# Residual stream kept transposed, with the FFN result added to the output rows by accumulating scatters

## What is computed

```
# conditioning: each sequence b has its own 32x32 matrix, picked by index
c = einsum('bct,bcd->bdt', x, weights[subjects])
# attention on c: 32 heads of 16, rope on q and k, causal softmax over 32 positions
q, k, v = c @ wq.T, c @ wk.T, c @ wv.T
x1 = x + attention(rope(q), rope(k), v) @ wo.T
# a linear layer with 8 low-rank experts of rank 16, two of them picked per token
logits = x1 @ Wr.T + 5 * onehot(language)
gates = softmax over the top 2 of logits
x2 = x1 @ W.T + 2 * einsum('bter,bte,eor->bto', x1 @ A, gates, B)
# block FFN: 16 blocks of 32 features, of permuted features; the result goes back
t = x2[:, perm];  t = gelu(t by blocks @ up);  t = t @ down by blocks
out = x1 + t[:, argsort(perm)]
```

## Time and profile before

| | |
|---|---|
| median of 3 runs | 265.93 us (265.58 to 266.53) |
| profiled execution: its own time | 266.65 us |
| its span in the profile | 264.8 us |
| PE busy | 233.0 us, 88% |
| DVE, ACT, POOL busy | 163.5, 118.4, 91.9 us |
| DMA | 11.66 MB |

### The profile page before, as it was taken

One profiled execution on the slowest core, in us unless ns is written; L12 is line 12 of the kernel. 1 busy time (PEld: TensorE's weight loads), 2 busy tenths in 40 slices (PEclk: granted clock), 3 DMA queues, 4 the chain that ended last, 5 costly groups with the idle time before them and its releaser, 6 DMA issues.

```text
span 264.8 us, 5842 instructions
## 1 busy us (share of the span) xinstructions
PE 233.0 (88%) x2472; PEld 194.6 (73%) x2472; DVE 163.5 (62%) x328; ACT 118.4 (45%) x199; POOL 91.9 (35%) x76
## 2 busy tenths in 40 slices
PE   5999498997779999998989999989996888969775
PEld 5999376985558899876867999757685666739543
DVE  2651999999835778848437977484479704424313
ACT  3332456640603234868024248681324599203470
POOL 8259763384920016768000058590001400000000
PEclk9999899997979999999999999999999579979999
DMA  7698421000000000000220000000100000020002
GB/s 229 215 339 280 149 50 57 2 0 0 4 0 0 2 2 1 4 2 0 82 79 2 2 0 2 0 2 26 57 2 0 0 4 0 2 79 2 0 0 79
DMA packets 7529, 11.66 MB, mean 44 GB/s; under 512 B 2032, under 2 KB 2704, under 8 KB 7504
## 3 DMA queue, kind: packets, MB, share of 16 engines
q1 hardware_dynamic: 6784, 9.81, 10.8%
q0 software_dynamic: 432, 1.48, 1.7%
q10 hardware_dynamic: 288, 0.01, 0.1%
HBM read 9.07 MB, written 2.23 MB: 43 GB/s over the span
## 4 chain that ended last, share of the span: by engine, by line
PE 50%; DVE 19%; ACT 11%; DMA 10%; issue 7%; POOL 2%; DVEq 0%; ACTq 0%; SPq 0%; POOLq 0%
PE ps_F L474 7%; PE ps_F L476 7%; PE ps_F L475 6%; PE ps_F L680 6%; ACT pbd L818 5%; PE ps_A L474 5%; PE ps_A L476 4%; PE ps_A L475 4%; DMA rows<-kr 3%; PE ps_F L653 3%; ACT act L900 2%; DMA wg<-rows 2%; PE ps_S L548 2%; PE ps_F L566 2%; PE ps_A L501 1%
## 5 line engine op out<-in xcount | busy, mean ns | idle before, releaser
L436 POOL TENSOR_TENSOR pr<-pr,small 128x512 f32<-128x512 f32 x16 | 16.6, 1048 | 86.7 <-DVE small L1103 86.7
L818 ACT ACTIVATE pbd<-pr 32x512 f32<-32x512 f32 x64 | 40.2, 628 | 9.8 <-DVE pr L1109 5.0
L818 ACT ACTIVATE x<-ps_F 128x512 fp32r<-128x512 f32 (+1 forms) x22 | 13.1, 597 | 49.1 <-PE ps_F L587 35.5
L412 POOL TENSOR_TENSOR rot<-rot,cst 128x512 f32<-128x512 f32 x14 | 18.0, 1288 | 20.2 <-DVE rot L1059 20.2
L1081 DVE TENSOR_TENSOR kbd<-kr,cst 128x512 f32<-128x512 f32 x16 | 20.8, 1342 | 3.6 <-POOL kr L416 3.5
L427 POOL TENSOR_TENSOR kbd<-kr,cst 128x512 f32<-128x512 f32 x16 | 21.1, 1346 | 2.7 <-PE ps_F L483 2.6
L474 PE MATMUL ps_A<-wvT,xc 128*128 128x512 f32 x32 | 14.8, 464 | 5.8 <-DVE wvT L1018 3.5
L1011 DVE TENSOR_TENSOR y<-ps_S,y 128x512 fp32r<-128x512 f32 x8 | 5.5, 688 | 22.8 <-ACT y L818 22.7
L474 PE MATMUL ps_A<-xc,wqT 128*128 128x256 f32 x64 | 18.2, 284 | 1.3 <-DVE xc L1011 1.3
L474 PE MATMUL ps_A<-xc,wkT 128*128 128x256 f32 x64 | 18.3, 286 | 0.0
L474 PE MATMUL ps_F<-x,w2T 128*128 128x256 f32 x64 | 18.3, 286 | 0.0
(11 more groups left out here) (156 smaller groups left out, 643.8 us busy)
## 6 DMA issues: line engine op xcount, KB each, us to landing
xs<-in_x SPq DMA_DIRECT2D x4, 512.0 KB, 4.5
out<-xs SPq DMA_DIRECT2D x3, 512.0 KB, 2.8
pbd<-in_L_attn_wq SPq DMA_DIRECT2D x2, 512.0 KB, 5.2
act<-in_L_attn_wk SPq DMA_DIRECT2D x1, 1024.0 KB, 5.6
act<-in_L_attn_wv SPq DMA_DIRECT2D x1, 1024.0 KB, 8.6
act<-in_L_attn_wo SPq DMA_DIRECT2D x1, 1024.0 KB, 8.0
out<-xs SPq DMA_DIRECT2D x2, 256.0 KB, 2.0
x<-in_L_cond_A SPq DMA_DIRECT2D x1, 256.0 KB, 8.2
```

The source lines that it names most:

```text
L412: pool.tensor_tensor(rv, rv, con("sin").unsqueeze(1).to_broadcast([P, 2 * N // T, T]), ALU.mult).then_inc(rot_sin, 1)
L436: pool.tensor_tensor(pr[:, i, :, :], pr[:, i, :, :], mx[:, i, :].unsqueeze(2).to_broadcast([P, NH // 2, T]), ALU.mult).then_inc(normed, 1)
L818: return sc.activation(dst, src, ACT.Copy)
```

## The change

The host gives x a second time, transposed (`xT`), and turns the output back. The output tensor in memory has one row for each feature of a group: 4 x 512 rows of 256 tokens.

1. `wo_proj(g, i)` makes features 256 i to 256 i + 255 for all 256 tokens of the group: 24 products of 256 columns in place of 12 of 512. It needs the split attention output of both tiles. `add_x` adds into `xt` (two buffers, loaded by SP); `x1_out` and `x1_lo` split `xt` directly. `turn_x1` goes.
2. SP writes `xt` (x1) to the output. The FFN result `y` is copied from PSUM by ACT alone, and POOL adds it to the output rows in memory with four indirect DMAs a group (`add_rows`), by `row_at`, the permuted row numbers. `unpermute`, `unperm`, `y_lo` and `add_ffn` go.
3. x of groups 2 and 3 is loaded without waiting for output. `attn` now lies in the buffer `xc`.
4. In the setup: ACT splits wv ahead of its part of `blocks(1)`; ACT's copies of wo move ahead of `v_out(0, 0)`; the lo part of wo moves from DVE to POOL, behind the first two `norm`; POOL clears `pbd` behind its first `k_blocks`; DVE's order in pass 0 is another, with the splits of the two small weights at its end.
5. In pass 3 PE runs all of pv before the second half of `ffn_down`, and then both halves of `wo_proj`.
6. `lora_down` takes the first two chunks of x1 for both of its products, then the other two.

```diff
+            def load_xt(g):
+                sp.dma_start(xt[:, g % 2, :, :], xT[g]).then_inc(d_xt[g], 16)
...
             for g in range(G):
-                for t in range(GT):
-                    wait_read(sp, Fi(g, "UN", t))
...
+                for i in range(2):
+                    wait_read(sp, Fi(g, "WO", i))
+                sp.dma_start(out_d[g], xt[:, g % 2, :, :]).then_inc(d_x1[g], 16)
...
+            def wo_los():
+
+                for h in range(2):
+                    rows = slice(2 * h, 2 * h + 2)
+                    pool.wait_ge(w_hi, W_AT["wo"] + h + 1)
+                    pool.tensor_tensor(WT["wo"][:, 1, rows, :], raw["wo"][:, rows, :],
+                                       WT["wo"][:, 0, rows, :].bitcast(F32), ALU.subtract).then_inc(wo_lo, 1)
+
+            def add_rows(g):
+
+                pool.wait_ge(rows_ready, G)
+                pool.wait_ge(d_x1[g], 16)
+                for c in range(KC):
+                    wait_read(pool, S_down(g, c // 2))
+                    pool.indirect_dma_start(out=out, out_offset=bass.IndirectOffsetOnAxis(
+                                                ap=row_at[:, g, c:c + 1], axis=0),
+                                            in_=y[:, c, :], in_offset=None, compute_op=ALU.add
+                                            ).then_inc(d_out[g], 16)
...
-            def wo_proj(g, t):
-                it = Fi(g, "WO", t)
-                wait_free(pe, it)
-                wait_read(pe, PVi(g, t))
...
+            def wo_proj(g, i):
+                it = Fi(g, "WO", i)
                 wait_free(pe, it)
                 for t in range(GT):
+                    wait_read(pe, PVi(g, t))
+                W, o = WT["wo"], attn
+                for h in range(2):
+                    c = 2 * i + h
+                    for k in range(KC):
+                        last = mm3(bank(it)[:, N * h:N * h + N],
+                                   W[:, 0, k, P * c:P * c + P], W[:, 1, k, P * c:P * c + P],
+                                   o[:, 0, k, :], o[:, 1, k, :], k == 0, k == KC - 1)
...
             w_his("wk", raw["wk"], WT["wk"], (d_w["wk"], None))
+            w_his("wv", raw["wv"], WT["wv"], (d_w["wv"], None))
             blocks(1)
-            w_his("wv", raw["wv"], WT["wv"], (d_w["wv"], None))
...
-            def x1_out(g, t):
-                split_hi(Fi(g, "XT", t), x1[:, 0, :, P * t:P * t + P], x1_hi)
+            def x1_out(g, i):
+
+                wait_read(sc, Fi(g, "WO", i))
+                copy(x1[:, 0, 2 * i:2 * i + 2, :], xt[:, g % 2, 2 * i:2 * i + 2, :]).then_inc(x1_hi, 1)
```

More of the change, by code:

```diff
@@ L41 @@
 HG = HC // 2
-XS = 3
+XS = 2
 MASKED = -1.0e30
@@ L77, in constants, with build @@
     return c
-def build(nc, x, who, wcond, wq, wk, wv, wo, w2b, wr, wa, up, down, perm, consts, cols, rows, out):
+def build(nc, x, xT, who, wcond, wq, wk, wv, wo, w2b, wr, wa, up, down, perm, consts, rows, out):
     ctx = ExitStack()
@@ L669, in ffn_down @@
                     last.then_inc(s_full(it), 1)
-            def unpermute(g, t, halves=(0, 1)):
-                it = Fi(g, "UN", t)
-                for i in halves:
-                    if i == 0:
-                        wait_free(pe, it)
-                    wait_read(pe, S_down(g, i))
-                    for c in (2 * i, 2 * i + 1):
-                        for part in range(2):
-                            last = pe.matmul(bank(it)[:, :], y2[:, part, c, P * t:P * t + P], unperm[:, c, :],
-                                             start=(c == 0 and part == 0), stop=(c == KC - 1 and part == 1),
-                                             skip_group_check=True)
-                    if i == 1:
-                        last.then_inc(s_full(it), 1)
             def keep_busy(n):
@@ L774, in _ @@
                     pv(g, 0, 3)
+                    for c in range(KC):
+                        pv(g, 1, c)
                     ffn_down(g - 1, 2)
@@ L777, in _ @@
                 wo_proj(g, 0)
-                if not more:
-                    pv(g, 1, 0)
-                    pv(g, 1, 1)
-                    unpermute(g - 1, 0)
-                    turn_x1(g, 0)
-                    pv(g, 1, 2)
-                    pv(g, 1, 3)
-                    unpermute(g - 1, 1)
                 wo_proj(g, 1)
-                if more:
-                    turn_x1(g, 0)
                 if g == 0:
@@ L808, in _ @@
                 ffn_down(G - 1, c)
-            for half in range(2):
-                for t in range(GT):
-                    unpermute(G - 1, t, (half,))
         @block.scalar
@@ L965, in _ @@
                     y_out(g - 1, 0)
-                if more:
-                    probs_block(g, 1, 0)
-                o_out(g, 0)
-                if more:
+                probs_block(g, 1, 0)
+                if more and g:
+                    o_out(g, 0)
                     v_out(g + 1, 0)
-                if g:
                     y_out(g - 1, 1)
-                if not more:
-                    probs_block(g, 1, 0)
+                elif more:
+                    v_out(g + 1, 0)
+                    o_out(g, 0)
+                else:
+                    o_out(g, 0)
                 probs_block(g, 1, 1)
@@ L977, in _ @@
                     v_out(g + 1, 1)
-                else:
-                    x1_out(g, 0)
                 o_out(g, 1)
-                if more:
-                    x1_out(g, 0)
-            x1_out(G - 1, 1)
+                if not more:
+                    y_out(g - 1, 1)
+                x1_out(g, 0)
+                x1_out(g, 1)
             h_out(G - 1)
```

226 lines of the change are left out of this document (101 added, 125 removed).

## The result

The changed kernel took **253.69 us** (median of 4 runs, 253.23 to 254.5) against 265.75 (264.51 to 266.53) for the kernel before on the same chip: ratio 0.9553, 95% interval 0.9508 to 0.9598. The profiled execution took 253.85 with a span of 252.1 us; before, 266.65 with 264.8. 12.1 us went. The forecast was 16.9, and the missing part is what the experiments are about.

What follows compares the result with a forecast made beforehand. PE, busy 88% of the span, was taken as the bound, with DVE and POOL deciding up to 86 us. Terms -12.2 - 4.1 - 3.3 - 0.5 + 1.5 + 1.7 = -16.9 gave 249.7 profiled, 249.0 median; range 244 to 257.

Steps and rivals of the forecast that it cites:

- The clock: PE at three ends of passes: new idle time lowers the clock at one of the three, +1.7 us.
- clock falls at every end: Rival: clock falls at every pass end and stays low in the last group, two more times 1.7, 252.5 us; chance 0.14.
- Group 0: Setup and group 0: reordered setup and earlier splits start `lora_down` at 74.0 instead of 86.25, -12.2 us.
- the first scores come about 5.0 us earlier: Setup: with wv first, DVE's subtractions fill idle times and PE's k, ended by 26.1, bounds group 0's last rope.
- wo on POOL at nothing: Setup: wo's two operations, 5.2 us together, hide in POOL's wait of 6.22 us, costing 0.
- The POOL rival: Group 0: POOL's wo operations and DVE's block each other, the ropes start late, +7, 256 us; chance 0.12.
- Pass 1: End of pass 1: `unpermute` traded for a wait -1.9, transposes -0.9, x's wait -1.27; together -4.1 us.
- Pass 2: End of pass 2: -1.9 and -0.9 as in pass 1, and -0.5 of waiting before `add_x` transposes; -3.3 us.
- Last group: Pass 3: savings from `unpermute` and transposes go back to waits and a lowered-clock `wo_proj`; -0.5 us, between -3 and +2.
- The end: After y's last copies: four adding scatters, costed as gathers of 0.94 us on POOL and 5.0 to land; +1.5 us.
- The fast rival: Whole kernel: no clock fall, and the scatters land in 3 us; 245.4 us, chance 0.10.
- the slow ones: Adding scatters hold POOL 7 us each, 272 us, chance 0.04; or group 0's gain is lost, 266 us, chance 0.04.

Runs made afterwards that it cites:

- experiments 5: The changed kernel with the lo part of wo subtracted by DVE again instead of POOL; 254.53 us, ratio 0.9608.
- experiments 9: The changed kernel with DVE's first subtraction for wv moved ahead of the second rope in the setup; 252.01 us, ratio 0.9454.
- experiment 6: The changed kernel with scatters that write y instead of adding it, so the output lacks x1; 255.45 us, ratio 0.9568.
- experiment 1: The changed kernel with eight filler products of 512 columns ahead of `wo_proj` in groups 0 to 2; 250.47 us, ratio 0.9393.
- 10: The kernel of experiment 7 with DVE's first subtraction for wv moved ahead of the second rope; 245.91 us, ratio 0.9183.
- experiment 4: The kernel before, old layout, with most setup edits (wv early, wo's subtraction on POOL, small weights and `unpermuter` later); median 262.67 us.
- experiment 7: The changed kernel with `cond` ahead of `wo_proj` in groups 0 and 1, fillers in group 2 and the last group; 245.95 us, ratio 0.9282.
- experiment 8: The kernel of experiment 7 with the first half of y copied by DVE in the last group; 246.27 us, ratio 0.9255.

## Why the prediction was right, and where it was off

The direction and the range held; the time came 4.7 us above the forecast. In spans: 4.3 by the terms below, of 4.2 measured.

- **The clock: +1.7 forecast, +4.5 measured (2.8 off), the largest miss.** The step that failed was "I take one fall of three": it fell at all three. The mechanism, its place and the price of one (1.5 to 1.7 against 1.7) were right; the count was a guess. At the ends of passes 1 and 2, 2.02 us of idle time follow a pv that itself waited 1.16 us, and there the clock fell six times of six, in the changed kernel and in experiments 5 and 9. At the end of group 0 no 1.16 us wait stands ahead, and it fell in one of four executions (the changed kernel's; not in those of 5, 6 and 9); whether the third fall belongs to the kernel or to that execution isn't known. The rival "clock falls at every end" gave 252.5 and was the closest; its other half, the slow `wo_proj` of the last group, didn't come.
- **Group 0: -12.2 forecast; -8.95 measured, and -8.95 - 1.5 = -10.45 without the fall (1.8 off).** The step was "the first scores come about 5.0 us earlier": they came 2.7 earlier (34.49 against 37.21). PE's k ended at 26.1 as forecast, but it wasn't the bound. I had not priced that DVE's subtractions now lie beside POOL's ropes: here 1.24 us of waiting and 1.81 us for an operation that takes 0.68 alone; in experiment 1 no wait, but two subtractions of 2.10 and 2.34 us in place of 1.21. The loss is the same either way (experiments 9 and 10). From there on the account held: `wo_proj` at 66.67 is 2.2 late, the same lateness.
- **wo on POOL at nothing: right.** 4.78 us against 5.2, ended before it was in the way. The POOL rival priced a real mechanism, but it struck in the setup, not there.
- **Pass 1, -4.1: -2.60 with 1.5 of clock taken out is -4.1. Pass 2, -3.3: -1.51 - 1.5 = -3.0.** Trading `unpermute` for a bare wait of 2.0, the transposes for nothing and x's wait for nothing came out as costed. (The forecast wrote 3.9 for 128.84 - 125.01, which is 3.8.) With 1.7 for a fall they would be -4.3 and -3.2, so the exact hit has luck in it.
- **Last group: -0.5 forecast, -2.72 measured.** The failed step was "`wo_proj` runs at a lowered clock": it took 220.09 - 214.24 = 5.85 us at 0.98, though PE had idled 4.16 and 1.16 us shortly before. The slow stretch lay ahead of it, over two pv and an `ffn_down` of 1.93 us each. That makes 1.6 of the 2.2; and `wo_proj` started 35.5 us behind the marker of pass 2, where the forecast's 228.5 is 36.7 behind it. (The two together are 2.8: the forecast's own 236 and its -0.5 didn't quite fit each other.)
- **The end: +1.5 forecast, +3.1 measured.** The mechanism held, and the sizes were off on both sides: 1.56 us of POOL and not 0.94 for each scatter (+1.9 over three), a start 0.92 us behind the copy where I had 0.05 (+0.9), against a last landing that was half a microsecond shorter and a first copy that ended 0.4 us earlier behind the marker, though an `ffn_down` at half clock had cost it 0.8. The plain gather was the wrong row for POOL's part: an addition costs the engine too. As to landing, the Trainium skill (DMA: Bandwidth & Descriptors, Anatomy of one DMA, SWDGE path) gave an estimate of 2.3 us. The scatter without an addition measured 2.4 and agrees, and the one with it measured 3.9.
- **The fast rival (245.4, no fall) and the slow ones** (7 us of POOL per scatter, nothing gained) didn't come. Without falls at the pass ends the changed kernel stands at 250.47 (experiment 1), not 245.4, for the setup, the tail and the slow stretch of the last group are still as above.

**Open:** why the same 2.02 us lowered the clock at the end of group 0 in one execution and not in three; why a wait of 3.39 us ahead of `wo_proj` was followed by slow products before and one of 3.16 us in experiment 4 was not; what held ACT in experiment 6; what lies in the 0.9 us between y's copy and the scatter (0.8 without the addition).

## What to carry to other kernels

When an edit takes work out of PE's stream, ask what that work covered: `unpermute` had covered a 2.0 us wait for a split, and the bare wait cost its length and then 1.5 us of slow products behind it, so that of 3.8 us only 0.3 were won. Put work that is needed anyway into such a hole (in the traces `cond` gave 2.0 and 1.5 us more than fillers at two places), and fillers only where there is none. When DVE and POOL both read SBUF with two operands at once, the loss here was the same whichever engine paid it, and moving one piece moved the collision; so count the time of both engines' operations together and don't rely on order alone. And before a marker's shift is read as a gain, take out where the execution began and what its clock did: both were worth a microsecond and more here.

## What the runs showed of the hardware

- An adding indirect scatter of 128 rows takes POOL 1.56 us against 0.97 without addition, and lands 3.9 us after its issue against 2.4.
- `wo_proj` as 48 products took 5.52 to 5.73 us at full clock and 7.24 to 7.26 with one fall; the level lay at half for only part of it (0.53 to 0.65 over the first 3.4 us).
- The clock at one place differs between executions: the first half of the last `ffn_down` took 1.07 us in experiment 7 and 1.94 in experiment 8, with the same products before it on PE.
- Operations of DVE and POOL with two inputs in SBUF lengthen each other: 1.29 us alone and 2.2 to 2.3 beside the other on POOL, 1.21 and 1.5 to 2.8 on DVE.
